# One order of scores and weighings in every cycle of a batched attention kernel

## What is computed

```python
xn = (x - mean(x)) / sqrt(var(x) + 1e-5)
# attention: LayerNorm again with ln_w, ln_b -> z; 16 heads of 16
q, k, v = z @ Wq.T + bq, z @ Wk.T + bk, z @ Wv.T + bv
q, k = rope(q), rope(k)
attn = softmax(q @ k.T / sqrt(16))           # per batch and head, 1024 x 1024
attn_block = xn + (attn @ v) @ Wo.T + bo
# experts: 8 experts, each takes its 256 best rows of every batch
affinity = softmax(xn @ gate_w)
gating, index = top_k(affinity.T, 256)
h = silu(xn[index] @ Wg[e]) * (xn[index] @ Wu[e])
moe_block = scatter_add(index, (h @ Wd[e]) * gating)
out = x + attn_block + moe_block
```

## Time and profile before

| | |
|---|---|
| median of 3 runs | 1776.63 us |
| lowest, highest | 1771.92, 1778.85 us |
| the profiled execution, its time | 1778.85 us |
| its span, first to last instruction | 1777.1 us |
| mean granted clock of TensorE | 0.984 of full speed |
| ACT busy | 1198.3 us, 67% |
| exponentials (L757) | 1024, 974.9 us busy |
| weighings (L967) | 4096 matmuls |

### The profile page before, as it was taken

One profiled execution on the slowest core, in us unless ns is written; L12 is line 12 of the kernel. 1 busy time (PEld: TensorE's weight loads), 2 busy tenths in 40 slices (PEclk: granted clock), 3 DMA queues, 4 the chain that ended last, 5 costly groups with the idle time before them and its releaser, 6 DMA issues.

```text
span 1777.1 us, 28942 instructions
## 1 busy us (share of the span) xinstructions
PE 1697.7 (96%) x11240; PEld 970.3 (55%) x11240; DVE 1034.8 (58%) x2056; ACT 1198.3 (67%) x1416; POOL 509.2 (29%) x480
## 2 busy tenths in 40 slices
PE   4499999999999999999999999899999999999997
PEld 4133344433434434434434433248888888888886
DVE  8646457456557558557647649747555454555543
ACT  3399988898898898898898889873333333333322
POOL 2101201111111111112111100025565656565653
PEclk9699999999999999999999999899999999999998
DMA  3634566558457457465475465535453434444332
GB/s 115 189 57 92 143 123 132 128 129 153 112 123 156 118 131 142 117 151 119 112 151 108 106 155 93 100 94 137 96 102 54 101 55 101 89 67 90 64 55 30
DMA packets 113458, 195.03 MB, mean 110 GB/s; under 512 B 20880, under 2 KB 59152, under 8 KB 113296
## 3 DMA queue, kind: packets, MB, share of 16 engines
q1 hardware_dynamic: 84112, 142.48, 36.2%
q0 software_dynamic: 29184, 50.35, 14.7%
HBM read 116.22 MB, written 76.55 MB: 108 GB/s over the span
## 4 chain that ended last, share of the span: by engine, by line
PE 87%; DVE 7%; DMA 2%; ACT 1%; issue 1%; POOL 1%; SPq 0%; DVEq 0%; ACTq 0%; POOLq 0%
PE o_ps L967 24%; PE score L1041 20%; PE score L953 18%; PE side L840 5%; PE score L1053 5%; PE o_ps L1053 3%; PE side L850 3%; PE side L1053 2%; PE side L881 2%; PE side L824 2%; PE score L1028 1%; DVE stats L1089 1%; DMA k_stack<-k_parts 1%; ACT probs L757 1%; DVE rot L1190 1%
## 5 line engine op out<-in xcount | busy, mean ns | idle before, releaser
L757 ACT ACTIVATE probs<-score 128x1024 f32<-128x1024 f32 x1024 | 974.9, 1037 | 144.5 <-PE score L953 142.7
L967 PE MATMUL o_ps<-probs,v_ones 128*32 128x512 f32 x4096 | 508.5, 605 | 7.8 <-DVE o_sb L1385 7.5
L953 PE MATMUL score<-q_stack,k_stack 50*128 50x512 f32 x2048 | 408.1, 463 | 17.3 <-DMA k_stack<-k_parts 11.1
L953 PEld LDWEIGHTS score<-q_stack,k_stack 50*128 50x128 f32 x2048 | 165.4, 186 | 362.2 <-ACT probs L757 299.5
L741 ACT ACTIVATE probs<-score 128x512 f32<-128x512 f32 x128 | 76.6, 598 | 335.0 <-PE score L1041 335.0
L668 POOL DMA_INDIRECT out<-probs,rot x128 | 204.3, 1596 | 212.2 <-DVE probs L1348 182.9
L967 PEld LDWEIGHTS o_ps<-probs,v_ones 128*32 128x32 f32 x4096 | 101.7, 109 | 229.0 <-issue 146.7
L1333 DVE TENSOR_TENSOR probs<-score,probs 128x512 f32<-128x512 f32 x128 | 88.5, 691 | 208.4 <-PE score L1041 180.9
L646 POOL TENSOR_TENSOR square<-qk 128x512 bf16<-128x512 f32 x56 | 77.2, 1407 | 398.8 <-DVE qk L1196 398.8
L1041 PE MATMUL score<-parts,q_stack 128*128 128x512 f32 x640 | 158.2, 389 | 0.0
L657 POOL DMA_INDIRECT qk<-xn_rows,rot x128 | 134.3, 1049 | 38.3 <-issue 29.3
(11 more groups left out here) (247 smaller groups left out, 2556.4 us busy)
## 6 DMA issues: line engine op xcount, KB each, us to landing
q_parts<-parts SPq DMA_DIRECT2D x16, 1024.0 KB, 4.3
k_parts<-parts SPq DMA_DIRECT2D x16, 1024.0 KB, 7.3
q_stack<-q_parts SPq DMA_DIRECT2D x62, 256.0 KB, 7.3
k_stack<-k_parts SPq DMA_DIRECT2D x62, 256.0 KB, 9.5
q_stack<-q_parts SPq DMA_DIRECT2D x66, 128.0 KB, 8.1
k_stack<-k_parts SPq DMA_DIRECT2D x66, 128.0 KB, 8.8
o_sums<-o_sb SPq DMA_DIRECT2D x256, 32.0 KB
num<-o_sums SPq DMA_DIRECT2D x32, 256.0 KB
```

The lines of the kernel that those rows point to most:

```text
L757: act.activation(probs[probs_of(s)][:, 2 * i:2 * i + 2, :], score[ring_of(p)][:, :, :], ACT.Exp, scale=SCALE).then_inc(exp_done, 1)
L953: last = pe.matmul(score[ring_of(p)][:, w, :], k_stack[par][rows, i, kt * P:(kt + 1) * P], q_stack[par][rows, i, qh * HALF:(qh + 1) * HALF ...
L967: last = pe.matmul(o_ps[j * KEYS_W:(j + 1) * KEYS_W, :], v_ones[par][:, kt, j, :], probs[probs_of(s)][:, j, :], start=kt == 0, stop=kt == ...
```

## The change

The helper `weigh_past` goes, and its two calls become one loop ahead of the odd step's scores. What was done in cycles with a job is now done in all.

```diff
-        def weigh_past(b, s, prev):
-
-            if s >= 0:
-                weigh(b, s)
-            elif prev is not None:
-                weigh(prev, STEPS + s)
-
@@ in attend(b, nxt, prev), for each cycle c
                 scores(b, 2 * c)
-                weigh_past(b, 2 * c - 2, prev)
-                if c in jobs.by_cycle:
-                    weigh_past(b, 2 * c - 1, prev)
+                for s in (2 * c - 2, 2 * c - 1):
+                    if s >= 0:
+                        weigh(b, s)
+                    elif prev is not None:
+                        weigh(prev, STEPS + s)
                 scores(b, 2 * c + 1)
-                if c not in jobs.by_cycle:
-                    weigh_past(b, 2 * c - 1, prev)
                 if c in jobs.by_cycle:
```

## The result

The changed kernel takes 1790.86 us (median of 4, 1789.08 to 1792.96), the one before 1775.14 (median of 4). The ratio is 1.0088, 95% interval 1.0063 to 1.0113: slower by 15.7 us, where 8.4 was forecast. The time lies 0.9 above the range. A second series of the changed kernel gave 1791.69 and a ratio of 1.0091 (1.0066 to 1.0117). The two profiled executions are closer: 1791.62 against 1778.85, 12.8 apart.

The account below looks back on a forecast made before the run. The ring of three score buffers was taken to set 3.96 us beside short jobs, ACT 3.66 in batch 7's job-free cycles. 10.77 (batches 0 to 6) - 2.4 (batch 7) = +8.4: 1787.2, by the median 1785.0; range 1777 to 1790.

Parts of the forecast that it names:

- The loop and its prices: Changed cycles take 3.96 us, set by the ring of three score buffers; last weighing to next batch's first, 4.88.
- The sum of rows 2: Cycle loop: two weighings 1.85, exponential's start 0.60, its run 1.03, buffer reuse 0.05, next weighing 0.43: 3.96 us.
- 10.77: Batches 0 to 6: 1.57 us for batch 0's cycles plus 9.20 for the batch boundaries up to batch 6.
- 0.70: Entry to batch 7: the new order in cycle 31 of batch 6 costs 0.70 us more.
- The second rival: In 50 changed cycles, PE's saved mode changes count, 0.14 us each: -7, 1769.6; chance 0.12.
- the third: Rival: waits later in the batch take up the boundary slips, only batch 7 counts: -2.4 us, 1774.2; chance 0.08.
- the part on batch boundaries: Turns between batches: 4.88 us, then cycles 0 and 1 at 3.96 each, 12.80 together; all boundaries add 9.20.
- The base: The profiled execution, 1778.85 us, 2.2 above the median 1776.63; forecast 1787.2 from it, 1785.0 by the median.
- the entry's slip: Start of batch 7: the new order in cycle 31 of batch 6 makes it 0.70 us late.
- Batch 7: Early slip shrinks to 0.62 us, waits before cycles 16 and 21 shorten without clock fall, last weighing 2.4 earlier.
- The first rival: Batch 7: the clock falls after cycle 16 all the same: +10.5 us, 1787.1; chance 0.16.
- The fourth: Rival: batch 7's early slip passes in full, 3.0 us instead of 0.62: +10.8, 1787.4; chance 0.05.

Follow-up runs that it names:

- e4_pair: The changed kernel, but in cycles without a job the first pair of the odd scores goes ahead of the second weighing: 1776.47 us, ratio 1.0001.
- e2_bounds: The kernel before, with the new order only in cycles 30 and 31 of batch 0 and 0, 1, 31 of batches 1 to 6: 1790.69 us.
- b1_look: The kernel before, unchanged, run again for a second trace: 1776.39 us.
- b2_look: The kernel before, unchanged, run again for a third trace: 1773.78 us.
- e3_look: The kernel before, with the new order only in batch 7, run once more for its trace: 1773.25 us.
- e5_short: The kernel before, with the old order of job-free cycles also in cycles with a short job of batches 0 to 6: 1764.05 us, ratio 0.9933.
- e6_five: The kernel before, with the new order also in cycle 1 of batch 0 and cycles 4, 16, 25, 26 of batch 7: 1772.66 us, ratio 0.9979.
- e8_best: The kernel before, old order also beside short jobs of batches 0 to 6, new order in five job-free cycles of batches 0 and 7: 1761.17 us.
- e1_fill: The changed kernel with seven more matmuls on PE at the end of batches 0 to 6, their results unread: 1787.55 us, ratio 1.0064.
- a2_again: The changed kernel, unchanged, run again for a second trace: 1791.69 us, ratio 1.0091.

## Why the prediction was wrong

**The loop and its prices** were right. The sum of rows 2 (3.96) held in the changed cycles at full clock, save those of batch 7 in which something else is waited for (DVE's copy, the casts); 4.88 at the turn held too. 10.77 plus 0.70, that is 11.5, were forecast for the loops up to batch 7. In the first trace batch 7 begins 13.3 later; two clock falls before it added 3.3 and the start took off 1.4, which leaves 11.4. e4_pair shows that the loop and not a weighing moved ahead of scores is the cause. The second rival (mode changes, -7) fell with the result itself. e2_bounds refuted the third, that waits in the batches would take the slips up.

**The step that failed** is in the part on batch boundaries: "Cycles 0 and 1 then take 3.96 each." I had worked out that the last two exponentials hold PE up at the turn, and used the delay alone. I left out that PE, standing still 0.94 and 0.41 there, can lose its clock, and that the two weighings behind the gaps then take 3.19 in place of 1.85. I looked at the clock only in batch 7, where I took two waits, 1.25 without a fall and 2.96 with one, as the bounds. Two gaps that add up to 1.35 were enough, though not always: three of seven boundaries in the first trace, three in the second (one of them another), four in e2_bounds. In the seven traces with the old order at the turn (before, b1_look, b2_look, e3_look, e5_short, e6_five, e8_best) it fell at none of the 49. It cost 4.9 us in the first trace (3 x 1.65) and 4.3 in the second; e1_fill shows it by taking it away. Why a given boundary is hit and not another is open.

**The base** was the other part. The sum was made against one execution, and shifted by 2.2 to the median. That shift assumed that the 2.2 would be the same in both kernels. It is not: this execution of before was slow at the start and in the waits of batch 7, other executions of before are not, and the gain of the new order was counted against the slow ones. By the three traces of before, W(3) of batch 0 is 1.6 earlier on the mean than in the first; the new order gives 1.4 and 1.5 there, so nothing is won. From W(0) to W(31), batch 7 took 130.9, 129.5 and 126.5, mean 129.0; with the new order, without the slow cycle 0, 128.8 and 127.7: 0.7 is won, where 3.1 was counted from the entry's slip on. (The old order in e2_bounds and e5_short took 127.8 and 131.2, the new one in e1_fill and e3_look 129.1 and 127.7: again a spread wider than the gain.) With the means the terms are 11.5 (loops) + 4.6 (clock at the turn) + 0.1 (start) - 0.7 (batch 7) = 15.5. The part behind attention, with its own clock fall in two traces of three before and in one of two after, takes off 0.3: 15.2, and the mean spans differ by 15.1. The timed medians differ by 15.7.

Two small slips of the working changed nothing: 2 x 1.00 - 1.85 is 0.15, not 0.14, and the wait left before cycle 16 sums to 1.2, not 1.3.

**Batch 7** went step by step as forecast, in the first trace: copy to copy, both waits, no fall of the clock. Against the forecast of 3.1, and the first trace of before, it gave 3.2 in e3_look and in a2_again and 2.1 in the first trace of the changed kernel, in which PE got k_stack 0.95 later after the first copy of the batch than before (47.65 against 46.70). The first rival (a fall after cycle 16) did not occur with the new order in all of batch 7 in any of four traces (after, a2_again, e1_fill, e3_look), but two of these had no wait there to try it. The fourth (the slip of cycles 1 to 8 in full) did not either: in e3_look, which began batch 7 2.23 earlier than the first trace of before, the lead was down to 0.15 at W(8), back at 1.18 one cycle later, and 5.4 at W(31).

## What to carry to other kernels

Where buffers turn in a ring between two engines, add up the loop through both of them (work of one, start of the other, its duration, the release), not the busy time of either; whatever stands in front of the operation that feeds the other engine lengthens the loop, though it is no added work. A change that opens gaps on PE can have a second price, its clock, paid in the block behind the gap (here 1.1 to 1.65 us at 10 of 21 boundaries); look for it wherever an edit makes PE wait. And take two or three traces of the kernel before when the forecast is under one per cent: a gain counted against the slow part of one trace need not show in the median.

## What was not expected of the hardware

Gaps of 0.94 and 0.41 us, 0.5 of work apart, were followed by the halved clock at some batch boundaries (three of seven, twice; four of seven in e2_bounds). For the single waits of batch 7 their length does not tell by itself: 1.07, 1.25, 2.44 (e8_best) and 2.51 (e2_bounds) were not followed by a fall, 1.70 (e8_best), 1.71 (e6_five) and 2.14 (b1_look) were. The wait of 2.51 and the windows behind it:

```profile
1130.53 0.74 PE L953 MATMUL score<-q_stack,k_stack 50*128 50x512 f32 x4 [2.51 <-DMA k_stack<-k_parts]
...
1131.00:1133.00 2.00, 2.00 (x19) 0.61 (x20) 0.00 (x0) 1.88 (x3) 0.00 (x0) 1.00 1.11 342
1133.00:1135.00 2.00, 1.85 (x16) 0.54 (x13) 1.02 (x2) 2.00 (x4) 0.62 (x1) 1.00 1.11 151
```

So the prediction's reasoning from one wait of 1.25 and one of 2.96 had no firm bound to stand on. Matmuls of 32 columns that follow others of 32 columns started 0.11 us earlier than a transpose over the whole array did.
